# The score products of an mLSTM attention kernel on half the partitions, with a spread Q of half the columns

## Chip, cores and metric

The kernel runs on one core of a Trainium2 chip. The metric is the device time of one execution in microseconds (us); lower is better. The engines are TensorE (PE, its weight loads PEld), VectorE (DVE), ScalarE (ACT), GpSimd (POOL) and SyncE (SP); here SP issues nearly all the DMAs.

## What is computed

There are 16 sequences of 128 positions with 128 features and 8 heads of 16 features. A cell with decaying memory attends from the normalised x (queries) to ctx (keys and values), and a feed-forward network with weights of +1 and -1 follows. Cut to what matters:

```
q = layernorm(x); k = v = ctx
ig, fg = linear([q, k, v])                    # one number a head and position
cs = cumsum(log_sigmoid(fg))
log_D = cs[s] - cs[t] + ig[t]  for t <= s, else -inf
D = exp(log_D - max_t log_D)
C = (q_h @ k_h.T) / sqrt(16) * D              # 8 heads, 128 x 128 each
h = C / max(|sum C|, exp(-max log_D)) @ v_h
x = x + layernorm(h) * ln_scale
x = x + s2 * W2(relu2(s1 * W1(relu2(s0 * W0([y, -y])))))   # y = layernorm(x), widths 512, 512, 128
```

## The kernel before

The program is written out by hand: each engine has its own list, and semaphores tie the lists together. The 16 sequences are taken in four groups of four (g = n // 4). Of each group x (normalised to `xn`) and ctx are transposed on TensorE and copied out by ScalarE to `qcT`: partition = feature, with part 0 for the query and part 1 for the key. `gates(g)` makes the gate sums, `forget_min`, `gate_logs` and `gate_scans` the running maximum `max_row`, and a DMA through HBM spreads it to all partitions (`maxb`); for the first two sequences `spread_max` and `direct_mask` do that on TensorE and VectorE.

The scores of one sequence are two products, for heads 0 to 3 and heads 4 to 7. The stationary operand is the whole transposed key, 128 features. The moving operand is `q_heads`: in the columns of head h only the 16 partitions of head h hold the query, and all others hold zeros, so that a product over all 128 partitions gives the scores of single heads:

```
for half in range(2):
    pe.matmul(pS[:, 4 * half:4 * half + 4]..., qcT[:, g % 2, j, 1],
              q_heads[:, g % 2, j, 4 * half:4 * half + 4]..., start=True, stop=True)
```

Each half has its own PSUM bank of `pS`. An f32 product appears in the trace as two weight loads and two matmuls, so that one sequence has four of each at L367. `q_heads` has two buffers (group parity). GpSimd clears each once (L973, L975), and SP's `spread_heads(g)` writes the eight heads' blocks into it with eight DMAs (L292). The zeros around them stay.

The main loop has slots n = 0 to 22. In slot n TensorE makes `scores(n)` (which wait for `c_ready` of n - 1, as `pS` is single), `weigh(n - 1)` (the product with the values, L379, four products side by side on 32 columns of the array each), the turn of x2 (L396), the feed-forward products of older sequences (L416, L429, L437) and `turn_o(n - 1)` (L386). VectorE makes `make_c(n)` (scores times decay, L695), then the normalisers and norms of n - 1 to n - 3 and the low halves of the hidden layers (L789). ScalarE makes `decay(n + 1)` (eight exponentials, L549), `take_o` and the high halves (L572); GpSimd masks (L939), values, and the reciprocal roots (L907, L908, L917, L918).

Ahead of the loop VectorE clears two small gate weights (L817, L818), then runs `q_group(0)` (statistics of x, L637 and L645), `norm_group(0)` (four L654 that make `xn`; they wait for `q_rstd` from GpSimd's `q_scale(0, GB)`, L917 and L918), four small copies (L836 to L839), `q_group(1)`, the scalars of the network, `forget_min(0)` (L659), `norm_group(1)`, `gate_scans(0)` (L665 to L676). GpSimd makes the constants, then `q_scale(0, GB)`, clears the first half of `q_heads`, `q_scale(GB, GB)`, clears the second half, and copies values. TensorE turns `xn` (L328), runs `keep_busy` products without use (L444) and `gates(0)` (L338), and waits for `max_row` (L354).

Of the kernel before, what the change touches and what calls it, by code (L numbers as in the profile page):

```python
# [33 lines left out]
B, S, D = 16, 128, 128  # L34
NH = 8
DH = D // NH
GB = 4
# [60 lines left out]
def xattn_ffn(nc, x, ctx_in, igate_w, igate_b, fgate_w, fgate_b, ln_scale, k0, k1, k2, s0, s1, s2, running_max, out):  # L98
    with ExitStack() as stack:
        def sb(name, shape, dt=F32):  # L100
            return stack.enter_context(nc.sbuf_tensor(name, shape, dt))

        def ps(name, shape, dt=F32):
            return stack.enter_context(nc.psum_tensor(name, shape, dt))

        def sem(name):
            return stack.enter_context(nc.semaphore(name))
# [27 lines left out]
        ve_q = sb("ve_q", [128, GB])  # L135
        rs_q = sb("rs_q", [128, GB])
        qcT = sb("qcT", [128, 2, GB, 2, S])
        q_heads = sb("q_heads", [128, 2, GB, NH, S])
        f_min = sb("f_min", [128, S])
        f_abs = sb("f_abs", [128, S])  # L140
        f_exp = sb("f_exp", [128, S])
# [33 lines left out]
        pS = ps("pS", [128, NH, S])  # L175
# [10 lines left out]
        lns_loaded = sem("lns_loaded")  # L186
        ident_ready = sem("ident_ready")
        consts_ready = sem("consts_ready")
        q_heads_cleared = sem("q_heads_cleared")
        cleared = sem("cleared")  # L190
        gatew_turned = sem("gatew_turned")
        gatew_ready = sem("gatew_ready")
# [49 lines left out]
        def group_rows(dram, g):  # L242
            return dram[GB * g:GB * (g + 1)].rearrange("b s d -> s b d")
# [16 lines left out]
        def store(sp, f):  # L260
            sp.wait_ge(out_ready, f + 1)
            sp.dma_start(out[FG * f:FG * (f + 1)].rearrange("b s d -> s b d"),
                         outb[:, f % 2]).then_inc(out_stored[f % 2], 16)
# [3 lines left out]
        @block.sync  # L267
        def _(sp):
            def load_x(g):
                sp.dma_start(xs[:, GB * g:GB * (g + 1)], group_rows(x, g)).then_inc(x_loaded[g], 16)  # L270

            def load_ctx(g):
                sp.dma_start(cs_in[:, GB * g:GB * (g + 1)], group_rows(ctx_in, g)).then_inc(ctx_loaded[g], 16)

            load_x(0)
            for n, bias in enumerate((igate_b, fgate_b)):
                sp.dma_start(bias_in[:, n:n + 1], bias.rearrange("(h a) -> h a", a=1)).then_inc(gatew_loaded, 16)
            load_x(1)
            load_ctx(1)
            for k_dram, k_in in ((k0, k0_in), (k1, k1_in), (k2, k2_in)):  # L280
                sp.dma_start(k_in[:, :, :], k_dram.rearrange("(c p) n -> p c n", p=128)).then_inc(ffnw_loaded, 16)
            load_x(2)
            load_x(3)

            def spread_heads(g):

                sp.wait_ge(q_heads_cleared, g % 2 + 1)
                if g >= 2:
                    sp.wait_ge(scores_ready, 2 * GB * (g - 1))
                sp.wait_ge(turned_out, 2 * (g + 1))  # L290
                for h in range(NH):
                    sp.dma_start(q_heads[DH * h:DH * (h + 1), g % 2, :, h],  # L292
                                  qcT[DH * h:DH * (h + 1), g % 2, :, 0]).then_inc(heads_spread[g % 2], 16)

            for g in range(NG):
                spread_heads(g)

                p = g % 2
                sp.wait_ge(max_ready, g + 1)
                sp.dma_start(running_max[g], max_row[:, p, :]).then_inc(max_stored, 16)  # L300
                sp.wait_ge(max_stored, 16 * (g + 1))
                if g >= 2:
                    sp.wait_ge(exp_ready, GB * (g - 1))
                for j in range(GB):
                    if GB * g + j not in DIRECT:
                        sp.dma_start(maxb[:, p, j], running_max[g:g + 1, 32 * j:32 * j + NH].broadcast_to(
                            [128, NH, S])).then_inc(max_spread[p][j], 16)
                if g == 0:
                    load_ctx(2)
                    load_ctx(3)  # L310
            for f in range(NF):
                store(sp, f)
            for p in range(2):
                sp.wait_ge(out_stored[p], 16 * (NF // 2))

        @block.tensor
        def _(pe):
# [40 lines left out]
            def scores(n):  # L358
                g, j = divmod(n, GB)
                if j == 0:  # L360
                    pe.wait_ge(heads_spread[g % 2], 16 * NH * (g // 2 + 1))
                if n == 0:
                    pe.wait_ge(direct_masked, 2)
                for half in range(2):
                    if n >= 1:
                        pe.wait_ge(c_ready, 2 * (n - 1) + half + 1)
                    pe.matmul(pS[:, 4 * half:4 * half + 4].rearrange("p h s -> p (h s)"), qcT[:, g % 2, j, 1],  # L367
                              q_heads[:, g % 2, j, 4 * half:4 * half + 4].rearrange("p h s -> p (h s)"),
                              start=True, stop=True).then_inc(scores_ready, 1)

            def weigh(n):
# [95 lines left out]
            turn(1, 1)  # L467
            turn(1, 0)
            scores(0)
            gates(1)  # L470
            for n in range(SLOTS):
                g, k = divmod(n, GB)
                prepare = n < B and g + 1 < NG
                early, late = ffn_of_slot(n)
                if prepare and k == 0 and n > 0:
                    gates(g + 1)
                if 0 < n < B:
                    scores(n)
                if prepare and (k == 1 and g > 0 or n == 2):
                    turn_am(g + 1)  # L480
                if k == 3 and g + 2 < NG:
                    turn(g + 2, 1)
                if 0 <= n - 1 < B:
                    weigh(n - 1)
                if 0 <= n - 4 < B:
                    turn_x2(n - 4)
                if k == 3 and g + 2 < NG:
                    turn(g + 2, 0)
                for f, m in early:
                    ffn(f, m)  # L490
                if 0 <= n - 1 < B:
                    turn_o(n - 1)
                for f, m in late:
                    ffn(f, m)
# [124 lines left out]
        def _(dve):  # L619
            own = [0]  # L620

            def mark(ins):

                own[0] += 1
                ins.then_inc(dve_own, 1)
                return own[0]

            def step(ins):
                dve.wait_ge(dve_own, mark(ins))
# [184 lines left out]
            def gate_cols(part):  # L814
                return pF[0][0:D, 0, 2 * NH * part:2 * NH * (part + 1)].rearrange("p (n h) -> p n h", n=2)

            step(dve.memset(wq[:, :, :], 0.0))  # L817
            dve.memset(wkv[:, :, :], 0.0).then_inc(cleared, 1)  # L818
            dve.wait_ge(cleared, 1)
# [29 lines left out]
            for n in range(SLOTS):  # L849
                g, k = divmod(n, GB)  # L850
# [46 lines left out]
        def _(pool):  # L897
            own = [0]

            def step(ins):  # L900
                own[0] += 1
                ins.then_inc(pool_own, 1)
                pool.wait_ge(pool_own, own[0])
# [6 lines left out]
            def q_scale(n, count=1):  # L910
                if n >= B:
                    return
                e = n % GB
                pool.wait_ge(q_stats, n + count)
                if n >= GB:
                    pool.wait_ge(xn_ready, n + count - GB)
                step(pool.tensor_scalar(ve_q[:, e:e + count], mv_q[:, e:e + count, 1], LN_EPS, None, ALU.add))  # L917
                pool.tensor_tensor(rs_q[:, e:e + count], ve_q[:, e:e + count],  # L918
                                   minus_half[:, :].broadcast_to([128, count]), ALU.pow).then_inc(q_rstd, count)

            def take_values(n):
                if n >= B:
                    return
                g, j = divmod(n, GB)
                if j == 0:
                    pool.wait_ge(ctx_loaded[g], 16)
                if n >= 2 * GB:
                    pool.wait_ge(pv_ready, n - 2 * GB + 1)
                pool.tensor_copy(vals[:, g % 2, j, :, 0:DH], cs_in[:, n].rearrange("p (h d) -> p h d", d=DH)).then_inc(vals_ready, 1)  # L929
# [39 lines left out]
            step(pool.memset(vals[:, :, :, :, DH:VW], 0.0))  # L969
            pool.memset(vals[:, :, :, :, ONE:ONE + 1], 1.0).then_inc(consts_ready, 1)  # L970
            pool.wait_ge(consts_ready, 1)
            q_scale(0, GB)
            pool.memset(q_heads[:, 0], 0.0).then_inc(q_heads_cleared, 1)  # L973
            q_scale(GB, GB)
            pool.memset(q_heads[:, 1], 0.0).then_inc(q_heads_cleared, 1)  # L975
            take_values(0)
            take_values(1)
            q_scale(2 * GB, GB)
# [35 lines left out]
```

## Time and profile before

| | us |
|---|---|
| three runs | 138.19, 136.32, 137.94 |
| median | 137.94 |
| the profiled execution: span | 136.3 |
| its own time (the lowest of the three, equal to its span) | 136.32 |
| PE busy | 113.8 |
| DVE busy | 107.7 |
| ACT busy | 78.5 |
| POOL busy | 67.7 |

A row of the profile names the line, the engine, the operation and its output and inputs; "x4" is the number of instructions merged in it. Matmuls are pipelined, so a row's busy time is longer than the spacing from start to start. The granted clock is 1.00 where TensorE has its full 2.4 GHz and 0.50 where it has 1.2 GHz.

### The profile page before, as it was taken

Reading aid. Unit: us, or ns where it says so; the run is one execution under the profiler, and the core shown is the slowest. Engines: PE = TensorE matmul, PEld = TensorE weight load, DVE = VectorE, ACT = ScalarE, POOL = GpSimd, SP = SyncE. Lnnn points to the kernel's source line nnn. Section 1 sums busy time; section 2 is a strip of 40 time slices with the busy share of each in tenths; the row PEclk is TensorE's granted clock in tenths of the full one; section 3 lists DMA queues with packets and bytes.
Section 4 is the critical chain, followed back from the end, with each engine's and each line's share of the span. In section 5 each row is a group of like instructions: output and inputs, shape, how many; then the busy total and the mean of one; then the engine's idle time right before and its main releaser. Section 6 shows DMA issues by size and latency. Waiting matters only on the chain.

```text
span 136.3 us, 3303 instructions
## 1 busy us (share of the span) xinstructions
PE 113.8 (83%) x1087; PEld 80.2 (59%) x1087; DVE 107.7 (79%) x346; ACT 78.5 (58%) x226; POOL 67.7 (50%) x138
## 2 busy tenths in 40 slices
PE   5915929796888476999999999999999989989960
PEld 5805829543454233466857758658567577777850
DVE  0389797899998999976599799879969969874541
ACT  3011352997488578394959779498497433345220
POOL 6392953323768768738081846935823504540000
PEclk9975799999999997799999999999999999999997
DMA  3792123963693329800121691100100100101101
GB/s 109 196 253 65 33 42 100 273 153 60 237 311 84 55 48 332 261 16 0 34 42 25 281 342 38 41 0 5 38 0 5 38 0 0 46 2 38 38 5 38
DMA packets 13537, 12.56 MB, mean 92 GB/s; under 512 B 2112, under 2 KB 11728, under 8 KB 13520
## 3 DMA queue, kind: packets, MB, share of 16 engines
q1 hardware_dynamic: 12384, 12.00, 30.4%
q10 hardware_dynamic: 1136, 0.35, 1.1%
q8 instruction: 9, 0.15, 0.4%
q14 instruction: 8, 0.07, 0.2%
HBM read 9.99 MB, written 1.31 MB: 83 GB/s over the span
## 4 chain that ended last, share of the span: by engine, by line
POOL 34%; issue 29%; DVE 14%; PE 12%; ACT 6%; DMA 3%; POOLq 1%; DVEq 0%; ACTq 0%
POOL maxb L939 9%; POOL rs_x L908 6%; DVE xn L654 6%; POOL rs_h L908 5%; PE pF L437 5%; POOL x2p L958 5%; ACT dmat L549 3%; DMA xs<-in_x 3%; POOL ve_x L907 2%; POOL ve_h L907 2%; PE pF L416 2%; POOL vals L929 2%; POOL rs_q L918 2%; PE pF L354 2%; PE pG L338 1%
## 5 line engine op out<-in xcount | busy, mean ns | idle before, releaser
L549 ACT ACTIVATE dmat<-maxb,aT 128x128 f32<-128x128 f32 x128 | 39.2, 391 | 0.4 <-DVE maxb L684 0.4
L367 PE MATMUL pS<-q_heads,qcT 128*128 128x512 f32 x64 | 31.4, 613 | 0.8 <-DVE cmat L695 0.8
L437 PE MATMUL pF<-h,w 128*128 128x256 f16 x256 | 30.3, 273 | 0.0
L437 PEld LDWEIGHTS pF<-h,w 128*128 128x128 f16 x256 | 24.7, 98 | 2.7
L789 DVE SCALAR_TENSOR_TENSOR h<-pF,h 128x512 f16<-128x512 f32 x32 | 20.9, 680 | 5.9 <-ACT h L572 5.9
L572 ACT ACTIVATE h<-pF 128x512 f16<-128x512 f32 x32 | 18.1, 592 | 9.9 <-PE pF L437 9.8
L958 POOL TENSOR_TENSOR x2p<-x,x2p 128x128 f16<-128x128 f32 x16 | 6.8, 428 | 30.4 <-ACT x2p L564 30.4
L695 DVE SCALAR_TENSOR_TENSOR cmat<-pS,dmat 128x512 f32<-128x512 f32 x32 | 20.5, 681 | 0.0
L367 PEld LDWEIGHTS pS<-q_heads,qcT 128*128 128x128 f32 x64 | 11.3, 196 | 10.1 <-issue 8.1
L939 POOL TENSOR_SCALAR_AFFINE_SELECT maxb<-maxb 128x1024 f32<-128x1024 f32 x14 | 15.6, 1112 | 2.8 <-DMA maxb<-running_max 2.8
L558 ACT COPY oT<-pO 128x256 f32<-128x256 f32 x16 | 5.9, 369 | 13.4 <-PE pO L379 13.4
L379 PEld LDWEIGHTS pO<-cmat,vals 128*32 128x32 f32 x256 | 6.2, 109 | 10.5 <-issue 9.6
L654 DVE TENSOR_SCALAR xn<-xs,mv_q,rs_q 128x128 f32<-128x128 f32 x16 | 11.0, 1080 | 1.6 <-POOL rs_q L918 1.6
L379 PE MATMUL pO<-cmat,vals 128*32 128x128 f32 x256 | 10.3, 278 | 1.7 <-issue 1.6
L510 ACT COPY qcT<-pG 128x512 f32<-128x512 f32 x8 | 4.6, 580 | 12.2 <-PE pG L328 12.2
L416 PE MATMUL pF<-w,h 128*128 128x128 f16 x128 | 8.6, 219 | 1.8 <-DVE h L789 1.8
L908 POOL TENSOR_TENSOR rs_x<-ve_x,minus_half 128x1 f32<-128x1 f32 x16 | 9.4, 585 | 1.3
L429 PE MATMUL pF<-x2T,w 128*128 128x256 f16 x64 | 9.1, 290 | 1.0 <-DVE x2T L775 1.0
L908 POOL TENSOR_TENSOR rs_h<-ve_h,minus_half 128x1 f32<-128x1 f32 x16 | 8.9, 554 | 1.3
L444 PE MATMUL pF<-ident 128*128 128x128 f32 x44 | 7.9, 346 | 1.7 <-POOL ident L962 1.7
L386 PE MATMUL pO<-ident,oT 128*128 128x128 f32 x32 | 6.5, 286 | 3.0 <-ACT oT L558 3.0
L416 PEld LDWEIGHTS pF<-w,h 128*128 128x128 f16 x128 | 7.4, 98 | 2.4 <-DVE h L789 2.4
(93 smaller groups left out, 174.1 us busy)
## 6 DMA issues: line engine op xcount, KB each, us to landing
maxb<-running_max SPq DMA_DIRECT2D x14, 512.0 KB, 5.3
xs<-in_x SPq DMA_DIRECT2D x4, 256.0 KB, 5.9
q_heads<-qcT SPq DMA_DIRECT2D x32, 32.0 KB, 2.0
out<-outb SPq DMA_DIRECT2D x8, 128.0 KB, 1.8
cs_in<-in_ctx SPq DMA_DIRECT2D x3, 256.0 KB, 6.2
cs_in<-in_ctx ACTq DMA_DIRECT2D x1, 256.0 KB, 4.2
k_in<-in_L_ffn_k SPq DMA_DIRECT2D x1, 256.0 KB, 5.8
running_max<-max_row SPq DMA_DIRECT2D x4, 64.0 KB, 1.6
```

The source lines that it names most:

```text
L367: pe.matmul(pS[:, 4 * half:4 * half + 4].rearrange("p h s -> p (h s)"), qcT[:, g % 2, j, 1], q_heads[:, g % 2, j, 4 * half:4 * half + 4].r ...
L379: last = pe.matmul(pO[32 * i:32 * i + VW, half], vals[:, n // GB % 2, n % GB, h], cmat[:, n % 2, h], start=True, stop=True)
L416: last = pe.matmul(bank[:, 0, D * j:D * (j + 1)], h2[:, k, part, S * j:S * (j + 1)], w2[:, k], start=(k == 0 and part == 0), stop=(k == FT ...
L437: last = pe.matmul(bank[:, u], w1[:, k, columns], h1[:, k, part], start=(k == 0 and part == 0), stop=(k == FT - 1 and part == 1))
L549: last = act.activation(dmat[:, n % 2, h], maxb[:, g % 2, j, h], ACT.Exp, bias=aT[:, g % 2, j, h:h + 1], scale=-1.0)
L572: act.activation(hidden(f, m, 0), ffn_place(f, m), ACT.Relu).then_inc(ffn_high, 1)
L654: dve.tensor_scalar(xn[:, n % (2 * GB)], xs[:, n], mv_q[:, n % GB, 0:1], rs_q[:, n % GB:n % GB + 1], ALU.subtract, ALU.mult).then_inc(xn_r ...
L695: dve.scalar_tensor_tensor(out=cmat[:, n % 2, part].rearrange("p h s -> p (h s)"), in0=pS[:, part].rearrange("p h s -> p (h s)"), scalar=Q ...
L789: dve.scalar_tensor_tensor(out=hidden(f, m, 1), in0=ffn_place(f, m), scalar=0.0, in1=hidden(f, m, 0), op0=ALU.max, op1=ALU.subtract).then_ ...
L908: return pool.tensor_tensor(dst, work, minus_half[:, :], ALU.pow)
L939: pool.affine_select(out=maxb[:, g % 2, j], in_=maxb[:, g % 2, j], compare_op=ALU.is_ge, fill=NEVER, base=0, pattern=[[0, NH], [1, S]], ch ...
L958: pool.tensor_tensor(x2p[:, n % 2, 1], x2[:, n % 2], x2p[:, n % 2, 0], ALU.subtract).then_inc(x2_low, 1)
```

## The change

The spread Q holds four head columns in place of eight: heads h and h + 4 share the columns h % 4, since their partitions (0 to 63 and 64 to 127) differ. Each half of the scores is a product over its own 64 partitions of key and spread Q. The buffer to be cleared has half the columns. Parity 0 is cleared by VectorE as its first instruction, parity 1 by GpSimd ahead of `q_scale(0, GB)`, each with its own semaphore. The eight DMAs of `spread_heads` carry as much as before.

```diff
-        q_heads = sb("q_heads", [128, 2, GB, NH, S])
+        q_heads = sb("q_heads", [128, 2, GB, NH // 2, S])
...
-        q_heads_cleared = sem("q_heads_cleared")
+        q_heads_cleared = [sem(f"q_heads_cleared{p}") for p in range(2)]
...
-                sp.wait_ge(q_heads_cleared, g % 2 + 1)
+                sp.wait_ge(q_heads_cleared[g % 2], 1)
...
-                    sp.dma_start(q_heads[DH * h:DH * (h + 1), g % 2, :, h],
+                    sp.dma_start(q_heads[DH * h:DH * (h + 1), g % 2, :, h % 4],
...
-                    pe.matmul(pS[:, 4 * half:4 * half + 4].rearrange("p h s -> p (h s)"), qcT[:, g % 2, j, 1],
-                              q_heads[:, g % 2, j, 4 * half:4 * half + 4].rearrange("p h s -> p (h s)"),
+                    rows = slice(64 * half, 64 * (half + 1))
+                    pe.matmul(pS[:, 4 * half:4 * half + 4].rearrange("p h s -> p (h s)"), qcT[rows, g % 2, j, 1],
+                              q_heads[rows, g % 2, j].rearrange("p h s -> p (h s)"),
                               start=True, stop=True).then_inc(scores_ready, 1)
...
+            dve.memset(q_heads[:, 0], 0.0).then_inc(q_heads_cleared[0], 1)
             step(dve.memset(wq[:, :, :], 0.0))
...
             pool.wait_ge(consts_ready, 1)
+            pool.memset(q_heads[:, 1], 0.0).then_inc(q_heads_cleared[1], 1)
             q_scale(0, GB)
-            pool.memset(q_heads[:, 0], 0.0).then_inc(q_heads_cleared, 1)
             q_scale(GB, GB)
-            pool.memset(q_heads[:, 1], 0.0).then_inc(q_heads_cleared, 1)
             take_values(0)
```

On GpSimd, from the last constant on, the kernel before has this order (`vals` are the values with their constant columns, `ve_q` and `rs_q` the variance and reciprocal root of x):

```order
L970 MEMSET vals 128x64
L917 TENSOR_SCALAR ve_q<-mv_q 128x4
L918 TENSOR_TENSOR rs_q<-ve_q,minus_half 128x4
L973 MEMSET q_heads 128x4096
L917 TENSOR_SCALAR ve_q<-mv_q 128x4
L918 TENSOR_TENSOR rs_q<-ve_q,minus_half 128x4
L975 MEMSET q_heads 128x4096
L929 COPY vals<-cs_in 128x8x16 x2
```

In the changed kernel the same place on GpSimd reads:

```order
L972 MEMSET vals 128x64
L974 MEMSET q_heads 128x2048
L919 TENSOR_SCALAR ve_q<-mv_q 128x4
L920 TENSOR_TENSOR rs_q<-ve_q,minus_half 128x4
L919 TENSOR_SCALAR ve_q<-mv_q 128x4
L920 TENSOR_TENSOR rs_q<-ve_q,minus_half 128x4
L931 COPY vals<-cs_in 128x8x16 x2
```

Two memsets of 4096 elements behind the reciprocal roots have become one of 2048 ahead of them.

On VectorE the program began, before the change, with the two gate weights and the statistics of x:

```order
L618 UNCONDITIONAL_BRANCH
L817 MEMSET wq 128x64
L818 MEMSET wkv 128x64
L637 BN_STATS st_q<-xs 128x6 x2
L645 BN_AGGR mv_q<-st_q 128x2
```

In the changed kernel the start of VectorE's program reads:

```order
L619 UNCONDITIONAL_BRANCH
L818 MEMSET q_heads 128x2048
L819 MEMSET wq 128x64
L820 MEMSET wkv 128x64
L638 BN_STATS st_q<-xs 128x6 x2
L646 BN_AGGR mv_q<-st_q 128x2
```

One memset of 2048 elements stands ahead of the rest. On TensorE, ScalarE and SP no instruction changes its place.

## Rows read from the trace of the kernel before

**Rows 1.** The page: busy time by engine, and the granted clock in 40 slices.

```profile
PE 113.8 (83%) x1087; PEld 80.2 (59%) x1087; DVE 107.7 (79%) x346; ACT 78.5 (58%) x226; POOL 67.7 (50%) x138
...
PEclk9975799999999997799999999999999999999997
```

**Rows 2.** Busy time by stretch, 26 us to 111 us (us from:to, length, busy by engine, clock, DMA share, GB/s).

```profile
26.11:36.98 10.87, 9.10 (x84) 4.20 (x82) 10.31 (x30) 7.88 (x27) 5.21 (x11) 1.00 0.53 152
...
47.59:54.87 7.28, 5.27 (x36) 2.74 (x35) 7.14 (x25) 5.85 (x21) 5.30 (x10) 0.87 0.63 184
...
60.59:68.08 7.49, 7.49 (x90) 5.33 (x89) 4.63 (x19) 5.65 (x17) 3.27 (x8) 1.00 0.09 15
68.08:79.36 11.28, 11.26 (x110) 7.84 (x107) 9.95 (x32) 8.55 (x29) 6.45 (x14) 1.00 0.39 133
79.36:90.09 10.73, 10.73 (x107) 7.42 (x105) 9.38 (x34) 8.05 (x25) 6.51 (x14) 1.00 0.31 105
90.09:100.81 10.72, 10.72 (x106) 7.41 (x105) 9.39 (x33) 8.04 (x25) 6.07 (x12) 1.00 0.05 14
100.81:111.50 10.69, 10.69 (x106) 7.31 (x104) 9.39 (x33) 6.19 (x17) 3.95 (x10) 1.00 0.05 14
```

**Rows 3.** Timeline of the start (start, us, engine, line, operation, count, idle time before and its releaser).

```profile
0.80 0.11 DVE L817 MEMSET wq<- 128x64 f32 x1 [0.80 <-PEq L1003]
...
3.74 0.21 POOL L970 MEMSET vals<- 128x64 f32 x1
4.62 0.49 DVE L637 BATCH_NORM_STATS2 st_q<-xs 128x6 f32<-128x128 f32 x2 [3.51 <-DMA xs<-in_x]
...
6.02 0.23 POOL L917 TENSOR_SCALAR ve_q<-mv_q 128x4 f32<-128x4 f32 x1 [2.07 <-DVE mv_q L645]
...
7.40 3.51 POOL L973 MEMSET q_heads<- 128x4096 f32 x1
7.49 4.08 DVE L654 TENSOR_SCALAR xn<-xs,mv_q,rs_q 128x128 f32<-128x128 f32 x4 [1.65 <-POOL rs_q L918]
11.49 0.15 DVE L836 COPY gate_b<-pF 128x2 f32<-128x2 f32 x1
11.62 0.72 PEld L328 LDWEIGHTS pG<-ident,xn 128*128 128x128 f32 x4 [4.61 <-DVE xn L654]
...
13.45 6.21 SPq L292 DMA_DIRECT2D q_heads<-qcT  x8
...
14.89 3.51 POOL L975 MEMSET q_heads<- 128x4096 f32 x1
...
15.53 0.35 DVE L659 TENSOR_SCALAR f_min<-pG,gate_b 128x128 f32<-128x128 f32 x1 [0.54 <-PE pG L338]
15.79 3.26 DVE L654 TENSOR_SCALAR xn<-xs,mv_q,rs_q 128x128 f32<-128x128 f32 x4
...
19.80 0.42 DVE L673 TENSOR_TENSOR_SCAN max_row<-a_row 128x128 f32<-128x128 f32 x1
```

**Rows 4.** All instructions that make xn, and the third group of four.

```profile
L654 DVE TENSOR_SCALAR xn<-xs,mv_q,rs_q x16: 328/340/3503, 7.5 to 49.3; 128x128 f32<-128x128 f32 x16
...
29.34 1.11 DVE L654 TENSOR_SCALAR xn<-xs,mv_q,rs_q 128x128 f32<-128x128 f32 x4
```

**Rows 5.** Granted clock by stretch, as in rows 2.

```profile
10.00:15.00 5.00, 3.38 (x36) 3.06 (x40) 4.61 (x25) 0.59 (x1) 2.29 (x4) 0.50 0.23 60
30.00:35.00 5.00, 3.73 (x25) 1.48 (x24) 4.72 (x15) 3.19 (x11) 2.27 (x5) 1.00 0.25 48
45.00:50.00 5.00, 3.20 (x26) 1.32 (x17) 4.86 (x17) 3.59 (x12) 4.08 (x9) 1.00 0.28 54
50.00:55.00 5.00, 3.15 (x29) 2.09 (x30) 4.93 (x20) 3.96 (x15) 3.39 (x7) 0.80 0.82 250
55.00:60.00 5.00, 4.72 (x36) 2.52 (x35) 4.13 (x15) 2.83 (x9) 3.34 (x7) 0.86 0.56 175
```

**Rows 6.** Timeline of TensorE around the scores of sequence 8.

```profile
67.53 0.40 PE L338 MATMUL pG<-qcT,wq 128*32 128x128 f32 x8
67.75 0.40 PE L338 MATMUL pG<-qcT,wkv 128*32 128x128 f32 x8
68.08 1.98 PE L367 MATMUL pS<-q_heads,qcT 128*128 128x512 f32 x4
...
69.04 1.02 PE L367 MATMUL pS<-q_heads,qcT 128*128 128x512 f32 x2
...
69.47 0.59 PE L367 MATMUL pS<-q_heads,qcT 128*128 128x512 f32 x1
70.00 0.65 PE L379 MATMUL pO<-cmat,vals 128*32 128x128 f32 x16
```

**Rows 7.** VectorE's wait for the turned output, once in two slots.

```profile
89.42 0.17 DVE L708 SCALAR_TENSOR_TENSOR den<-pO,em 128x8 f32<-128x8 f32 x1 [1.28 <-PE pO L386]
```

## The prediction, made before the changed kernel had run

> **What bounds the kernel now.** I read the page first. PE is busy 113.8 us of 136.3, DVE 107.7 [rows 1]. Two engines near 80% say little, so I cut the span into the stretches between the first score products of successive sequences. They fall into three parts. Up to 26 us one sequence of steps runs from x to the first scores. From 26 to 61 us DVE is nearly full (10.31 of 10.87 us, 7.14 of 7.28) while PE has gaps [rows 2]. From 61 to 111.5 us PE is full: 7.49 of 7.49 in one slot, then 10.73 of 10.73 in a pair of slots, where DVE has 9.38 [rows 2]. In that last part DVE waits once in a pair, 1.28 us, for the turned output of PE [rows 7]. What takes time off PE is therefore worth something from 61 us on, and at most until DVE is full. Behind 111.5 us no scores are left.
>
> The start holds the surprise. Four instructions L654 take 4.08 us at 7.49 and 3.26 us at 15.79, both times beside a memset of `q_heads` on POOL (7.40 to 10.91, 14.89 to 18.40) [rows 3]. The same four take 1.11 us at 29.34, and the sixteen range from 328 to 3503 ns [rows 4]. The longest, 3503 ns, has the length of the memset, 3.51 us: an xn instruction that meets the memset stands still until it ends. PE waits 4.61 us for the first xn [rows 3], and the second xn stands between `f_min` and the scans that make `max_row`. Both are on the path to the first scores.
>
> **The start, part by part.** The two memsets go from behind `q_scale`. The xn of group 0 then take 1.11 us, not 4.08: 2.97 us gained, done at 8.60. What is late next? DVE itself goes through copies, statistics and scalars: from 11.57 (end of xn) to the last scalar took it up to about 15.0, so 3.4 us, and it is ready for `f_min` at 12.0. PE's turn, copies and gates took 15.53 - 11.57 = 3.96 us at a granted clock of 0.50 [rows 3, 5], which gives 12.56, or near 12.0 if the clock stays up because the wait ahead of it is 1.6 us and not 4.61. I take 12.5 for `f_min`. The xn of group 1 follow: 1.11 us, not 3.26. Gain by `max_row`: 2.97 + 2.15 = 5.1 us, 5.6 with the clock up; I take 5.2. POOL's `rs_q` for it comes in time, for it moves with the statistics.
>
> What the moved memsets cost. POOL's one memset has half the elements: 3.51 / 2 = 1.76 us, from 3.95 to 5.71; its next work began at 6.02 [rows 3], so the wait for x hides it. If this cover were gone it would cost its 1.76 us less 2.07 us of idle time, nothing. VectorE's memset is not in the trace. By the nearest row, 64 elements in 0.11 us [rows 3], it is at most 32 x 0.11 = 3.5 us; at the pace of POOL's it is 1.76 us. DVE is idle from its first memsets to 4.62, waiting for x, so either ends by 4.6 and costs nothing; at worst some tenths of a us. The unknown is whether VectorE's memset stops POOL as POOL's stopped xn: POOL's constants would end up to 2.1 us later, the memset behind them at 7.8 in place of 5.71, and `ve_q` 1.8 us later than 6.02. And whether POOL's memset stops the statistics at 4.62: up to 1.1 us (5.71 - 4.62). I take 0 for both, since small DVE work with one SBUF input ran at its usual length beside the second memset (`f_min` 0.35 us at 15.53 [rows 3], though it reads PSUM).
>
> The Trainium skill (SBUF — State Buffer, Who interferes with whom) says that a DVE instruction in a two-port mode and a GpSimd instruction exclude each other for their whole length, and that a DVE instruction with at most one SBUF input outside those modes does not contend on trn2. The 3503 ns agree with the first half; no row here shows the second, which is what the new memset on DVE needs. The Trainium skill (VectorE: DVE Perf Modes, Zero memsets can be issued as uint32) gives a memset one cycle per element, an estimate of 2.1 us here at 0.96 GHz; the sum would not change by it.
>
> The DMAs of `spread_heads` start with `qcT` and so move 3 us earlier, but SP needs 6.21 us for the eight [rows 3]: from about 10.4 to 16.6. The store of `max_row` is queued behind them, ready at 15.1, so SP gains 3.7 us there, not 5.2. It feeds the mask of sequence 2, which POOL had done over 4 us before ScalarE needed it; I cost it at nothing, and at 1.5 us if that cover is gone.
>
> **The scores, part by part.** Four matmuls start at 68.08, 68.61, 69.04, 69.47; the pace is 0.43 us each and the four hold PE for 4 x 0.43 = 1.72 us a slot [rows 6]. Each alone does not get shorter: it streams 512 columns whatever its partitions. What can change is that the two halves use different rows of the array and different banks. The trace shows products beside each other on columns of the array: L338 has eight matmuls of 128 columns every 0.22 us (67.53 to 67.75), and L379 sixteen in 0.65 us [rows 6]. At the pace of the scores (0.43 us for 512 columns, so 0.11 for 128) eight in series would take 0.86 us. So four tiles run at once, and each tile's two passes in turn. If row tiles do the same, the scores take two paces, 0.86 us, a gain of 0.86; if the first pass of half 1 must wait until the last of half 0 has started, three paces, a gain of 0.43; if they stay in series, none. Against it stands a switch: from the last score (69.47 + 0.43 = 69.90) to L379 at 70.00 there are 0.10 us without streaming [rows 6], and a second such switch now comes ahead of the scores. Net gain a slot: 0.76, 0.33 or -0.10.
>
> The Trainium skill (TensorE: Matmul & The Clock Gate, Part 3) says that matmuls on distinct row groups run concurrently, and TensorEngine Tiling (Key Properties) that changing the tiling mode drains the engine. By these the net gain is the 0.76; the gap of 0.10 us agrees with the second, and of the first this trace shows only the column kind.
>
> In the PE-bound pairs: 10.73 - 2 x 0.76 = 9.21 us for PE, under DVE's 9.39. So DVE becomes the bound and the gain is at most 1.33 us a pair; with 0.33 a slot it is 0.66. No engine packs perfectly, and I take 0.95 a pair; over the four pairs from 68.08 to 111.50 that is 3.8. The slot from 60.59 has DVE at 4.63 of 7.49: 0.33 to 0.76, I take 0.6. The 34.5 us before are DVE-bound: between 0 and 6 x 0.76 = 4.6 us, I take 0.8. The clock: it was at 0.50 for some 3.4 us in all between 50 and 60 us (0.20 x 5 / 0.5 + 0.14 x 5 / 0.5), after a stretch with PE busy 3.20 of 5 us [rows 5]. PE will be idler there by up to 0.76 a slot, so more of this is likely: I take 0.7 us lost, from 0 to 3.4. Sum: 3.8 + 0.6 + 0.8 - 0.7 = 4.5 us.
>
> **Sum.** 5.2 + 4.5 = 9.7 us: 136.3 becomes 126.6 for an execution like the profiled one. That one is the fastest of the three; the median is 1.6 us above it, about what 3.3 us at half clock cost a full PE. I add half of that, 0.8: **127.4 us**.
>
> **Rivals.**
> - *Both gains in full.* DVE packs all pairs (4 x 1.33 = 5.3), the slot from 60.59 gives 0.76, the early slots 1.5, the clock costs nothing, and the start gives 5.6: 136.3 - 13.2 + 0.8 = 123.9. For it: DVE's waits are few. Against: each slot has hand-overs PE, ACT, DVE, PE.
> - *The halves stay in series.* The change does not do what it says; 12 slots at PE's bound pay 0.10 each. 136.3 - 5.2 + 1.2 + 0.8 = 133.1. For it: no product on part of the rows is in the trace, and f32 ones have two passes. Against: rows 6.
> - *The memset on DVE holds POOL.* `rs_q` comes 1.8 us later: 129.2.
> - *Slower: the clock.* Half of the array's rows idle in the scores, and PE has more gaps; the clock falls from 60 us on, where PE bounds. A us at 0.50 costs half a us of a full PE. From 127.4 to 140.7 (2% above the median) are 13.3 us: the clock must be at 0.50 for 26.6 of the 51 us up to 111.5. All of it would give 127.4 + 25 = about 152. For it: 0.50 from 10 to 15 us, after the 4.6 us wait. Against: 1.00 from 30 to 35 us with PE busy 3.73 of 5 us [rows 5].
>
> **Chances.** Forecast 0.62, both gains in full 0.15, in series 0.13, the memset 0.06, the clock 0.04 (of which 0.01 within 2%). Range 123.3 to 133.0: it takes in most of the first rival and up to the second. 2% is about what a measurement of this kernel can tell from no change, 135.2 to 140.7. Faster 0.94, same 0.03, slower 0.03.
>
> **What would show it.** No xn instruction over 0.4 us before 20 us; the first `max_row` near 15 us. Scores: starts of half 1 within a few ns of those of half 0 and the next product 1.0 us behind the first start (or 1.4, or 1.8). Pairs of slots of 9.5 to 10.1 us from 68 us on with DVE busy over 95%. A first `max_row` behind 17 us, scores of 1.8 us, or a clock under 0.9 behind 60 us would prove the forecast wrong.

## The result, and the profile after

The changed kernel takes 128.86 us (median of 5, 127.34 to 130.97) against 137.94 us; the ratio is 0.934 [0.926, 0.941]. The forecast was 127.4 us, 123.3 to 133.0. The span of the profiled execution fell from 136.3 to 125.6 us. Times here and in the table of the experiments are medians of all executions, while ratios and intervals leave out executions more than 1.5% above the fastest of their kernel (they keep 3 of 5 here, 3 of 6 in e1, 2 of 6 in e2, 3 of 4 in e4, 2 of 4 in e10 and all of the other runs), so a ratio is not the quotient of two medians.

The start. The timeline of the changed kernel's first 17 us (its lines stand one or two below those of before):

```profile
1.22 1.76 DVE L818 MEMSET q_heads<- 128x2048 f32 x1 [1.22 <-PEq L1004]
...
2.73 0.95 POOL L971 MEMSET vals<- 128x1024 f32 x1
...
2.94 0.11 DVE L819 MEMSET wq<- 128x64 f32 x1
...
4.01 1.80 POOL L974 MEMSET q_heads<- 128x2048 f32 x1
...
4.88 0.48 DVE L638 BATCH_NORM_STATS2 st_q<-xs 128x6 f32<-128x128 f32 x2 [1.64 <-DMA xs<-in_x]
...
6.19 0.23 POOL L919 TENSOR_SCALAR ve_q<-mv_q 128x4 f32<-128x4 f32 x1 [0.38 <-DVE mv_q L646]
...
7.67 1.11 DVE L655 TENSOR_SCALAR xn<-xs,mv_q,rs_q 128x128 f32<-128x128 f32 x4 [1.56 <-POOL rs_q L920]
...
12.11 0.34 DVE L660 TENSOR_SCALAR f_min<-pG,gate_b 128x128 f32<-128x128 f32 x1
12.37 1.11 DVE L655 TENSOR_SCALAR xn<-xs,mv_q,rs_q 128x128 f32<-128x128 f32 x4
...
14.42 0.42 DVE L674 TENSOR_TENSOR_SCAN max_row<-a_row 128x128 f32<-128x128 f32 x1
```

Both groups of xn take 1.11 us, where they took 4.08 and 3.26 [rows 3]; `max_row` starts at 14.42 in place of 19.80. POOL's 1.80 us fit ahead of 6.19, and the statistics of x beside them kept their length (0.48, before 0.49).

The gate products of the kernel before, then the turns of xn and the gate products of the changed one:

```profile
13.52 0.66 PE L338 MATMUL pG<-qcT,wq 128*32 128x128 f32 x8
```

```profile
8.84 1.11 PE L328 MATMUL pG<-ident,xn 128*128 128x128 f32 x4 [0.41 <-DVE xn L655]
...
10.72 0.43 PE L338 MATMUL pG<-qcT,wq 128*32 128x128 f32 x8 [0.31 <-ACT qcT L511]
```

The gate products ran at 0.50 before [rows 5] and at 1.00 here, so a part of the gain is the clock's. From the end of the first xn to `f_min` it was 15.53 - 11.57 = 3.96 us before and 12.11 - 8.78 = 3.33 now: 0.6 us.

The scores. TensorE around the scores of sequence 13, and the page's two lines on them (output and inputs, count, busy and mean ns, idle before):

```profile
86.41 0.38 PE L438 MATMUL pF<-h,w 128*128 128x256 f16 x2
86.72 1.13 PE L368 MATMUL pS<-q_heads,qcT 64*128 64x512 f32 x4
87.78 0.43 PE L380 MATMUL pO<-cmat,vals 128*32 128x128 f32 x8
```

```profile
L368 PE MATMUL pS<-q_heads,qcT 64*128 64x512 f32 x64 | 20.4, 662 | 1.8 <-DVE cmat L696 1.8
...
L368 PEld LDWEIGHTS pS<-q_heads,qcT 64*128 64x128 f32 x64 | 5.9, 192 | 6.1 <-DVE cmat L696 3.3
```

Four matmuls are busy for 1.13 us where they were for 1.98 [rows 6], and a single one is no shorter (662 ns in the mean; the shortest took 592 before and 589 after). In the trace's own records they start in pairs: 86.719 and 86.726, then 87.252 and 87.259. So the two halves run side by side, pass by pass, in this and 12 more of the 16 sequences. In sequences 1 to 3 half 1 starts 0.53 to 0.60 us behind half 0, and only two of the four passes run side by side.

The stretches of the changed kernel, cut where those of rows 2 were cut (us from:to, length, busy of PE, PEld, DVE, ACT, POOL, clock, DMA share, GB/s):

```profile
20.82:49.55 28.73, 20.54 (x204) 10.13 (x203) 26.43 (x90) 22.11 (x74) 18.26 (x39) 0.90 0.64 190
49.55:54.47 4.92, 4.64 (x42) 2.73 (x41) 4.68 (x18) 3.29 (x11) 3.18 (x7) 0.87 0.56 162
54.47:61.36 6.89, 6.89 (x90) 4.98 (x89) 4.45 (x17) 5.56 (x17) 3.28 (x8) 1.00 0.08 14
61.36:72.22 10.86, 9.99 (x111) 6.89 (x107) 10.03 (x32) 8.63 (x29) 6.44 (x14) 1.00 0.45 129
72.22:82.00 9.78, 9.56 (x105) 6.61 (x104) 9.71 (x35) 8.32 (x26) 6.51 (x14) 1.00 0.38 126
82.00:91.45 9.45, 9.45 (x105) 6.56 (x104) 9.08 (x32) 7.64 (x24) 6.06 (x12) 1.00 0.05 16
91.45:100.89 9.44, 9.21 (x103) 6.48 (x103) 9.37 (x33) 5.95 (x17) 3.95 (x10) 1.00 0.06 16
100.89:125.50 24.61, 18.71 (x206) 15.44 (x204) 14.95 (x42) 7.95 (x17) 5.54 (x14) 1.00 0.08 23
```

The kernel before over the first two of these stages:

```profile
26.11:54.87 28.76, 22.55 (x204) 11.44 (x203) 27.34 (x88) 21.96 (x73) 18.38 (x38) 0.97 0.57 163
54.87:60.59 5.72, 5.44 (x42) 3.19 (x41) 4.85 (x18) 3.55 (x12) 3.34 (x7) 0.87 0.51 160
```

Against these and [rows 2] the 10.8 us come from here:

| stretch | before | after | gain |
|---|---|---|---|
| up to the first scores | 26.11 | 20.82 | 5.29 |
| sequences 0 to 5 | 28.76 | 28.73 | 0.03 |
| sequence 6 | 5.72 | 4.92 | 0.80 |
| sequence 7 | 7.49 | 6.89 | 0.60 |
| pairs 8/9, 10/11, 12/13, 14/15 | 11.28, 10.73, 10.72, 10.69 | 10.86, 9.78, 9.45, 9.44 | 0.42, 0.95, 1.27, 1.25 |
| the rest | 24.8 | 24.7 | 0.1 |

Three places ask for an explanation. The first six sequences gained nothing. The pair 82.00 to 91.45 has PE full (9.45 of 9.45), not DVE (9.08). And in the early part the clock is lower: 0.90 over 28.73 us against 0.97 over 28.76, and at 0.50 throughout the stretch from 44.0 to 50.8.

### The profile page after: what moved, and what is told of

It is laid out like the page before. It is cut to its first block, busy times and chain, and to the rows that moved or that the text cites. A ratio compares the mean times of both kernels' runs of the same rounds, so it can differ in the third digit from the quotient of the medians.

```text
span 125.6 us, 3302 instructions
## 1 busy us (share of the span) xinstructions
PE 105.5 (84%) x1087; PEld 74.8 (60%) x1087; DVE 103.0 (82%) x347; ACT 78.1 (62%) x226; POOL 62.1 (49%) x137
## 4 chain that ended last, share of the span: by engine, by line
POOL 37%; issue 27%; PE 10%; DMA 8%; DVE 7%; ACT 4%; SPq 4%; POOLq 1%; DVEq 0%; ACTq 0%
POOL maxb L941 9%; POOL rs_x L910 7%; POOL rs_h L910 6%; PE pF L438 6%; POOL x2p L960 5%; SPq L292 4%; DMA xs<-in_x 3%; DMA maxb<-running_max 3%; POOL ve_x L909 2%; POOL ve_h L909 2%; PE pF L417 2%; POOL vals L931 2%; DMA running_max<-max_row 2%; POOL rs_q L920 2%; ACT dmat L550 2%
## 5 line engine op out<-in xcount | busy, mean ns | idle before, releaser
L438 PEld LDWEIGHTS pF<-h,w 128*128 128x128 f16 x256 | 24.7, 98 | 2.6
L368 PE MATMUL pS<-q_heads,qcT 64*128 64x512 f32 x64 | 20.4, 662 | 1.8 <-DVE cmat L696 1.8
L368 PEld LDWEIGHTS pS<-q_heads,qcT 64*128 64x128 f32 x64 | 5.9, 192 | 6.1 <-DVE cmat L696 3.3
L565 ACT CAST x2p<-x 128x128 f16<-128x128 f32 x16 | 4.7, 295 | 7.1 <-DVE x L769 7.1
```

The lines of the kernel that those rows point to most:

```text
L438: last = pe.matmul(bank[:, u], w1[:, k, columns], h1[:, k, part], start=(k == 0 and part == 0), stop=(k == FT - 1 and part == 1))
```

## Experiments

Medians and ratios to the kernel before, measured in the same rounds:

| run | us | ratio | interval |
|---|---|---|---|
| e1 start only | 133.62 | 0.965 | 0.957 to 0.973 |
| e2 rows only | 134.71 | 0.964 | 0.954 to 0.974 |
| e3 same rows | 142.02 | 1.036 | 1.029 to 1.044 |
| e4 clear back | 129.63 | 0.942 | 0.933 to 0.950 |
| e5 warm | 126.11 | 0.917 | 0.912 to 0.921 |
| e6 full clears | 130.53 | 0.949 | 0.943 to 0.955 |
| e7 switch, full height | 137.86 | 1.009 | 1.003 to 1.014 |
| e8 warm, same rows | 134.01 | 0.975 | 0.969 to 0.980 |
| e9 warm, on the kernel before | 136.71 | 1.000 | 0.994 to 1.006 |
| e10 the changed kernel again | 130.76 | 0.941 | 0.930 to 0.952 |
| e11 e5 again | 126.22 | 0.915 | 0.910 to 0.920 |

**e1, e2: the two parts alone.**

```diff
# e1, on the kernel before
+            dve.memset(q_heads[:, 0], 0.0).then_inc(q_heads_cleared[0], 1)
             step(dve.memset(wq[:, :, :], 0.0))
...
             q_scale(0, GB)
-            pool.memset(q_heads[:, 0], 0.0).then_inc(q_heads_cleared, 1)
             q_scale(GB, GB)
-            pool.memset(q_heads[:, 1], 0.0).then_inc(q_heads_cleared, 1)
             take_values(0)
             take_values(1)
+            pool.wait_ge(xn_ready, 2 * GB)
+            pool.memset(q_heads[:, 1], 0.0).then_inc(q_heads_cleared[1], 1)
```

```diff
# e2, on the kernel before
-                    sp.dma_start(q_heads[DH * h:DH * (h + 1), g % 2, :, h],
+                    sp.dma_start(q_heads[DH * h:DH * (h + 1), g % 2, :, h % 4],
...
+                    rows = slice(64 * half, 64 * (half + 1))
+                    pe.matmul(pS[:, 4 * half:4 * half + 4]..., qcT[rows, g % 2, j, 1],
+                              q_heads[rows, g % 2, j, 0:4]...,
```

Expected of e1: 

> The kernel before, with its full-height products and eight head columns; VectorE clears parity 0 first (4096 elements, as long as POOL's 3.51 us), POOL clears parity 1 only when both groups of xn are there. Theory (two separate gains, the start's is xn no longer stopped by POOL's memset): no xn over 0.4 us before 20 us, first max_row 5 us earlier than 20.2 (at 15.2: DVE's longer memset ends near 4.8 and may cost 0.3), scores unchanged at 1.29 us from first to last start, pairs of slots still 10.7 us; gain 5 us, ratio 0.964. Rival (the start is hidden behind something later, and the gain comes from the scores): ratio over 0.985.

Expected of e2: 

> The kernel before with only the products changed to 64 partitions each on four head columns; the buffer keeps its eight columns, so POOL's two memsets keep 4096 elements and their places. Theory: max_row at 20.2 as before, scores 0.54 us from first to last start, pairs of slots 9.4 to 9.8 us from the eighth on, little before; gain 4.5 to 5.5 us, ratio 0.962. Rival (the two gains overlap, for instance because the earlier start only moves waits): e1 and e2 together gain clearly more or less than the 9.1 us of the whole change.

Measured: 0.965 and 0.964. Their product is 0.930, and the whole change is 0.934 with its interval around it: two separate gains of about equal size, and within these intervals neither hides the other. The clock comes with the second part: all six executions of e2 had a mean granted clock of 0.906 to 0.973, those of e1 0.957 to 0.996. The instructions that make xn in e1 and e2 (count, min/median/max ns):

```profile
L654 DVE TENSOR_SCALAR xn<-xs,mv_q,rs_q x8: 336/342/349, 8.3 to 14.4; 128x128 f32<-128x128 f32 x8
```

```profile
L655 DVE TENSOR_SCALAR xn<-xs,mv_q,rs_q x8: 328/1416/3502, 7.5 to 18.7; 128x128 f32<-128x128 f32 x8
```

In e1 none is long; in e2 the stall is there with its 3502 ns. A detail of e1 missed: its `max_row` was done at 16.1, not 15.2. Its xn started at 8.28, 0.61 us behind the changed kernel's 7.67, as VectorE's memset is twice as long; and its gate products took 0.66 us where those of the changed kernel took 0.43, the other 0.64 us.

**e4, e6: what stalls xn, and what the halved buffer is for.**

```diff
# e4, on the changed kernel
-            pool.memset(q_heads[:, 1], 0.0).then_inc(q_heads_cleared[1], 1)
             q_scale(0, GB)
+            pool.memset(q_heads[:, 1], 0.0).then_inc(q_heads_cleared[1], 1)
# e6, on the changed kernel
-        q_heads = sb("q_heads", [128, 2, GB, NH // 2, S])
+        q_heads = sb("q_heads", [128, 2, GB, NH, S])
...
-                              q_heads[rows, g % 2, j]...,
+                              q_heads[rows, g % 2, j, 0:4]...,
```

Expected of e4: 

> The changed kernel with POOL's one memset of 2048 elements put back behind the first reciprocal root. Theory (an xn that meets a POOL memset stands until it ends): one xn of about 1750 ns, in place of 3503 before and 340 now; first max_row 1.7 us later than in the changed kernel (14.8 to 16.5); ratio 0.946. Rival (the stall has a fixed length, or xn was slow for another reason, such as its first use): one xn of 3500 ns, or none over 400 ns.

Expected of e6: 

> The changed kernel with its buffer at eight head columns, so both memsets have 4096 elements in their new places. Theory (the halved buffer matters only since it lets the memsets end before x comes): VectorE's ends near 4.7, POOL's near 7.5, the first reciprocal root 1.3 us later than in the changed kernel, first max_row at 16.1, ratio 0.943. Rival (the memsets run faster or are hidden anyway): first max_row at 14.8, ratio 0.934.

The start of e4, then the start of VectorE in e6:

```profile
7.52 1.80 POOL L975 MEMSET q_heads<- 128x2048 f32 x1
7.61 2.37 DVE L655 TENSOR_SCALAR xn<-xs,mv_q,rs_q 128x128 f32<-128x128 f32 x4 [1.65 <-POOL rs_q L920]
...
16.26 0.43 DVE L674 TENSOR_TENSOR_SCAN max_row<-a_row 128x128 f32<-128x128 f32 x1
```

```profile
1.64 3.47 DVE L818 MEMSET q_heads<- 128x4096 f32 x1 [1.64 <-PEq L1004]
5.08 0.11 DVE L819 MEMSET wq<- 128x64 f32 x1
```

The longest xn of e4 is 1798 ns: with half the memset, half the stall. The four together took 2.37 us and ended 1.20 us later than in the changed kernel (9.98 against 8.78). `max_row` started 1.84 us later (16.26 against 14.42); the other 0.64 us are the gate products, at 0.66 us in place of 0.43. The stall has the length of the memset, and the rival of a fixed length falls. In e6 the first of the two instructions for the reciprocal root came 1.3 us later (7.49 against 6.19), as expected, and `max_row` was done at 16.4 (expected 16.1); the ratio is 0.949 (expected 0.943). So moving the memsets gives most of the start's gain, and halving them another 1.3 us.

**e3: are the halves side by side?** This run changes what is computed: half 1 reads partitions 0 to 63 too, so heads 4 to 7 get the scores of heads 0 to 3.

```diff
-                    rows = slice(64 * half, 64 * (half + 1))
+                    rows = slice(0, 64)
```

Expected: 

> The changed kernel, but half 1 too reads partitions 0 to 63 of key and spread Q, so heads 4 to 7 get the scores of heads 0 to 3: same sizes, no second row tile. Theory (the gain comes from two row tiles beside each other): four starts 0.43 us apart, 1.29 us from first to last, pairs of slots 10.7 to 10.9 us, start as in the changed kernel; ratio 0.963. Rival (a product over 64 partitions is shorter by itself): 0.54 to 0.9 us from first to last and a ratio near 0.934.

The scores of e3 in the trace, its early part (in pieces and as a whole), and a late pair of slots:

```profile
93.23 1.98 PE L368 MATMUL pS<-q_heads,qcT 64*128 64x512 f32 x4
```

```profile
20.63:28.13 7.50, 6.23 (x60) 3.02 (x60) 6.43 (x18) 6.24 (x21) 2.36 (x6) 1.00 0.81 206
28.13:41.78 13.65, 12.91 (x58) 5.63 (x60) 8.08 (x32) 5.88 (x20) 8.03 (x18) 0.50 0.53 156
41.78:52.02 10.24, 7.83 (x83) 3.78 (x80) 9.71 (x37) 9.03 (x33) 6.50 (x15) 1.00 0.41 98
20.63:62.66 42.03, 37.45 (x243) 17.81 (x242) 31.44 (x107) 25.85 (x85) 22.17 (x48) 0.72 0.53 146
82.12:93.23 11.11, 11.11 (x105) 7.39 (x104) 9.47 (x33) 7.93 (x25) 6.43 (x14) 1.00 0.27 100
```

The series is back: 1.98 us for four, as before. That part of the theory stands, and its rival (shorter products) falls. The time does not: 142.02 us, a ratio of 1.036 where I had expected 0.963. The pair of slots is 11.11 us against 10.72: 0.20 us a slot more than before. And the early part, 42.03 us, ran at a mean clock of 0.72. All four executions had a mean granted clock of 0.894 to 0.915; those of e1, with the same series at full height, had 0.957 to 0.996.

PE's 37.45 busy us in that part say little, for a product at 0.50 is busy for longer. So I compare only stretches at the full clock. In e3 PE was busy 6.23 of 7.50 us before the clock fell at 28.13, and 7.83 of 10.24 us before it fell again at 52.02. Two stretches of e1:

```profile
28.13:40.00 11.87, 9.97 (x92) 5.25 (x90) 10.95 (x38) 9.19 (x30) 8.99 (x19) 1.00 0.66 195
45.00:55.00 10.00, 7.48 (x71) 4.59 (x71) 9.72 (x37) 7.71 (x27) 7.04 (x15) 1.00 0.71 218
```

With shares of busy time like those of e3 (9.97 of 11.87, 7.48 of 10.00) the clock of e1 stayed at 1.00.

**e7, e8: switches or half height?** e7 adds to e1 a product of 8 columns on 64 partitions, which the scores overwrite; e8 is e3 with products without use in TensorE's waits (below).

```diff
# e7, on e1
+                    if half == 0:
+                        pe.matmul(pS[:, 0, 0:8], qcT[0:64, g % 2, j, 1], q_heads[0:64, g % 2, j, 0, 0:8],
+                                  start=True, stop=True)
```

Expected of e7: 

> e1 (full-height products, clears off the path) plus one product of 8 columns on partitions 0 to 63 ahead of each sequence's scores, overwritten by them: it forces the array into the 64-row mode and out again. Theory (a switch costs 0.10 us without streaming and 0.11 us as the weight load behind it is bare; half-height products let the clock fall, not switches): slots from the eighth on 0.2 to 0.45 us longer than e1's 5.37, so about 2.5 to 5 us in all, mean clock 0.955 or more; ratio near 0.99. Rival (the switches are what drops the clock in e3): mean clock 0.89 to 0.92 and a ratio over 1.01.

Expected of e8: 

> e3 (both halves on partitions 0 to 63, so in series; heads 4 to 7 get the scores of heads 0 to 3) plus the products without use of e5. Theory (e3's 8 us over e1 are 15 switches of 0.19 us and the rest the clock at 0.50 in the early slots): mean clock 0.97 or more, 4 to 5 us faster than e3, ratio 1.0. Rival (e3 is slow for another reason): ratio 1.03 or more at a full clock, or the clock stays at 0.9 since half-height products themselves pull it down.

A late stretch of e7, and the early one of e8:

```profile
76.36:88.10 11.74, 11.74 (x109) 8.00 (x108) 9.81 (x33) 7.93 (x26) 6.49 (x14) 1.00 0.20 66
```

```profile
21.86:55.32 33.46, 32.02 (x292) 19.30 (x291) 31.75 (x104) 25.65 (x84) 21.56 (x45) 1.00 0.59 170
```

e7's pair is 11.74 us, 0.51 a slot over e1's 5.36: a switch in, the small product, and a switch out. I had expected 0.2 to 0.45 and a ratio near 0.99; it is 1.009. Its clock stayed at 0.967 to 0.993. So switching costs time of its own but does not pull the clock down. Of the differences between e3 and e1 that leaves the half height of products in series. In e8 the clock is back (0.967 to 1.000) and 8.0 us with it, 134.01 against 142.02; I had expected 4 to 5. From the first scores to those of sequence 7 it needs 33.46 us where e3 needs 42.03. A slot of it still has 5.55 us: the switch.

**e5, e9, e10, e11: the clock of the changed kernel.** e10 is the changed kernel once more. The edit of the others, the same on both kernels (e8 too), puts products without use into TensorE's waits:

```diff
                 if 0 < n < B:
+                    keep_busy({2: 6}.get(n, 0))
                     scores(n)
...
                 if 0 <= n - 1 < B:
+                    keep_busy({4: 3, 5: 3}.get(n, 0))
                     weigh(n - 1)
...
                 if 0 <= n - 1 < B:
+                    keep_busy({1: 2, 2: 2, 4: 6, 5: 2}.get(n, 0))
                     turn_o(n - 1)
```

Expected of e5: 

> The changed kernel plus products without use on TensorE where it waits in slots 1 to 5: two ahead of turn_o in slots 1, 2 and 5 and six in slot 4, six ahead of the scores of slot 2, three ahead of weigh in slots 4 and 5 (0.24 us each at full clock). Theory (the early slots leave TensorE so idle that its clock falls to 0.50, and the slot that meets it is 0.8 us longer): mean granted clock 0.985 or more in all runs, against 0.917 to 0.973 of the changed kernel, median about 127.3, ratio to before 0.925, runs closer together. Rival (DVE bounds there, the clock costs nothing): ratio 0.934 to 0.94 whatever the clock.

Expected of e9: 

> The kernel before plus the products without use of e5 in slots 1 to 5. Theory (the clock falls there because half-height products leave the array idle, so the kernel before, with full-height ones, loses little to it): gain of 0 to 1.7 us, since some of its executions have the clock at 0.50 once between 50 and 60 us; ratio 0.99 to 1.0. Rival (any filling of TensorE's waits helps by 2.8 us): ratio 0.98.

Expected of e10: 

> The changed kernel once more, on the chip and in the rounds of e9, for the comparison with e5: ratio 0.934 if the two chips agree, time 128 to 129 us, with a mean granted clock of 0.92 to 0.97.

Expected of e11: 

> e5 once more beside e10 on one chip: theory 2.5 us under e10 (ratio 0.916), rival (e5's chip was the faster one) within 0.5 us of e10.

The first six sequences of e5 and of e1, and 30 us of the early part of e10 (its profiled execution is the slowest of its four):

```profile
20.91:48.93 28.02, 24.58 (x251) 15.22 (x250) 25.82 (x86) 21.55 (x72) 18.12 (x38) 1.00 0.59 177
```

```profile
21.98:50.10 28.12, 21.75 (x204) 11.03 (x203) 26.01 (x85) 21.77 (x72) 18.08 (x38) 1.00 0.63 176
```

```profile
26.00:56.00 30.00, 22.42 (x173) 10.62 (x170) 25.32 (x86) 19.19 (x65) 19.84 (x42) 0.72 0.58 162
```

On one chip e10 took 130.76 us with a mean clock of 0.902 to 0.916 (expected: 128 to 129 us, 0.92 to 0.97), and e11 126.22 us with 0.985 to 0.994. By the ratios the filling is worth 2.4 us between two chips (0.917 in e5, 0.934 in the first result) and 3.5 us on one chip (0.915 in e11, 0.941 in e10), where I had expected 2.5. The same edit on the kernel before gave 1.000. So these us of the changed kernel go to the clock, and filling the waits wins them back: this version, with 0.917 and 0.915, is the fastest here. It also narrows the executions, to 125.56 to 126.75. My expectation of e5, 0.925, was too small a gain.

The kernel before loses to the clock too: its profiled execution had 0.87 over sequence 6. Its thirteen executions beside e9 fall into two groups, seven near 136.6 us and six near 138.2, and e9's ten do the same, six and four: the filling at these places did not change that.

What pulls the clock down in the changed kernel itself is not separated. From the first scores to the fall of the clock its PE was busy 16.42 of 23.17 us (20.82 to 43.99), and e1's 18.89 of 23.02 (21.98 to 45.00): it has more idle time, and it has half-height products, though side by side. e3 shows the second for products in series alone.

At a full clock the first six sequences take 28.02 us in e5 and, with full-height products, 28.12 in e1 (21.98 to 50.10). There the products side by side are worth 0.1 us. DVE is busy for 25.82 of the 28.02 us and is the nearest to a bound.

## Why the prediction was right, and where it was not

*The start, 5.2 us: right, measured 5.29.* The links held: xn 1.11 us twice, the memset of POOL hidden in the wait for x, `f_min` at 12.11. For that last the text had 12.0 if the clock stays up. It did not stay up: the four turns at 8.84 took 1.11 us, as the 1.12 before at 0.50, and it rose in time for the gate products at 10.72. The page's clock row has 9 in these slices all the same, so in the first us the length of the products is the better witness. That the size came out so well is luck in part. The same kernel had its first scores at 20.82 here and at 21.79 in e10 (e5 20.91 and e11 21.37, which differ only later), so the gain at the start is 4.3 to 5.3 us by when the clock rises. The SP queue held the store of `max_row` until 17.34, 2.5 us behind `max_row`. It feeds the mask of sequence 2, whose scores stood 6.98 us behind the first ones, before 7.09: the delay cost nothing.

*VectorE's memset, 0 us: right, with less room than the text gave.* Its row says 1.76 us from 1.22, but before the change the small memsets began at 0.80 [rows 3], and the next one now begins at 2.94. In e6, with twice the elements, the record starts at 1.64 and ends at 5.11. The late starts, 0.42 and 0.84 us behind 0.80, grow with the elements, so I take it that the engine works from 0.80 on and the record shows only the last part: 2.18 us and 4.31 us, an estimate of 1.06 ns an element. This pace agrees with the one cycle per element that the Trainium skill gives (VectorE: DVE Perf Modes, Zero memsets can be issued as uint32). It did not hold up POOL either: in e6 the memset of `vals` (2.73 to 3.68) lies wholly beside it and took 0.95 us, as in the kernel before. This agrees with what the Trainium skill (SBUF — State Buffer, Who interferes with whom) says of instructions with at most one SBUF input.

*The scores, two paces in place of four: right.* The starts in pairs and e3 show it. The Trainium skill (TensorE: Matmul & The Clock Gate, Part 3) says that matmuls on different tiles of the array run concurrently; for two row tiles of f32 this trace agrees, with starts 7 ns apart.

*The switch, 0.10 us: half of what it is.* e3's slots are 0.20 us over those of before. The last product ahead of the scores starts at 86.52, should stream for 0.11, and the first scores start at 86.72: 0.10 us without streaming. Then the second pair starts 0.53 us behind the first, not 0.43. The weight load of the first pass starts only with that pass (86.717), where without a switch it starts during the product before; I put the 0.10 us down to this. [rows 6] had this already: 68.08 to 68.61 is 0.53, and products on 32 columns stood ahead of these scores. I took the spacing without asking why one of three was longer. So PE needs 5.36 - 0.86 + 0.20 = 4.70 us a slot, 9.40 a pair, and the late pairs are 9.45. PE did not drop under DVE as the text said; the two ended level. In the pair at 82.00 PE is full and DVE waits 0.3 us, and in its two neighbours PE waits 0.2 us for DVE. The 3.8 us for four pairs came out as 3.89, and the slot from 60.59 as 0.60 (0.6). The 3.89 is a sum of unlike parts: the text had 0.95 for every pair, and they gave 0.42, 0.95, 1.27 and 1.25.

*The early slots, 0.8 us: right in size.* At a full clock it is 0.1 in the first six (28.02 in e5, 28.12 in e1) and 0.66 in the seventh (4.31 in e5, 4.97 in e1).

*The clock, 0.7 us lost: mis-sized.* Over the first seven sequences the changed kernel's profiled execution needed 1.3 us more than e5 (28.73 and 4.92 against 28.02 and 4.31). But the profiled execution of the kernel before needed 1.4 us more than e1, which has the same products (28.76 and 5.72 against 28.12 and 4.97). Between these two the clock cost nothing. By the ratios it cost the changed kernel 2.4 to 3.5 us, which e5 and e11 won back. The text reasoned from idle time alone. e3 and e7 show that the height of products in series counts as well; how much of it counts in the changed kernel stays open.

*The way from span to time: wrong.* I took the profiled execution for the fastest of the three, 136.32 us, since that equals its span. In the later executions the time stands 1.7 to 1.9 us above the span (127.34 for 125.6, 134.68 for 132.9, 136.43 for 134.6), so the profiled one took about 138.1. By the same sum it becomes 128.4, and the 0.8 us that I added for the median had no ground. That 128.4 lies near 128.86 is luck in part. The profiled executions differ by 10.8 us, 1.1 more than the 9.7 of the sum, of which 0.7 is the clock. Against this the profiled execution of the changed kernel is its fastest, 127.34, and lies 1.5 us under the median.

*The rivals.* Halves in series were priced at 133.1 us; e3 is that case and took 142.02. The price left out the clock: with the waits filled the same series took 134.01 (e8). It also had a switch at 0.10 us for 12 slots, where PE is full in nine (60.59 to 111.50) and the switch is 0.20. The range would have missed the 142.02. The clock rival had its place wrong: the fall comes where DVE bounds, not from 60 us on, where TensorE is full in both kernels and the clock stayed at 1.00.

## What to carry to other kernels

Some VectorE instructions can stand for the whole length of a GpSimd memset, and show as one instruction ten times its usual length. Here it was the f32 TENSOR_SCALAR that makes xn, and not the statistics of x. Look at the longest of a group, not its mean, and move long GpSimd work to where VectorE has nothing of that kind. Products on half the partitions that can be paired with the other half were worth half their time less 0.2 us for the extra switch of the array's mode in a slot, but only where TensorE bounds. Afterwards look at the granted clock in the parts where TensorE waits: products without use in those waits were worth 2.4 to 3.5 us here, a quarter or more of what the change gave.

## What the runs showed of the hardware that was not expected

- Half-height f32 products in series (e3) let the clock fall to 0.50 after 7.50 us with PE busy for 6.23 and again after 10.24 us with PE busy for 7.83; with full-height ones (e1) it stayed at 1.00 over 11.87 us with PE busy for 9.97 and over 10.00 us with 7.48. What the clock follows is more than busy time.
- A switch of the array's mode costs 0.10 us without streaming and another 0.10 us before the second pass, together 0.20 us a slot (e3's pair of slots 11.11 us against 10.72).
- The record of a long VectorE memset starts late, by 0.42 us for 2048 elements and 0.84 us for 4096 (e6) against the 0.80 us at which the engine's first memset started before. That the engine is taken from 0.80 us on is worked out from these two, not seen.
